# Macaron transformer block: transposes of the score maxima before or behind the products of probabilities and v

## What is computed

```python
x = x + 0.5 * ffn(layernorm(x))      # 256 -> 1024 -> 256, exact gelu, weights quantised to -1, 0, 1
x = x + attention(layernorm(x))      # 16 heads of 16, rotary positions, causal softmax
x = x + 0.5 * ffn(layernorm(x))

scores = einsum('bhqd,bhkd->bhqk', q, k) / 4;  scores = where(causal, scores, -inf)
attn = softmax(scores);  out = einsum('bhqk,bhkd->bhqd', attn, v)
```

## Time and profile before

| | us |
|---|---|
| median of 3 runs | 616.01 (614.93 to 616.15) |
| profiled execution, its own time | 616.8 |
| its span, first to last instruction | 614.8 |
| TensorE busy, matmuls | 572.6 (93% of the span) |
| VectorE busy | 459.6 (75%) |
| ScalarE busy | 344.7 (56%) |
| GpSimd busy | 231.7 (38%) |
| mean granted clock of TensorE, of full speed | 0.989 |

### The profile page before, as it was taken

How to read it: one execution, slowest core, us unless ns; L and a number is a source line. 1 busy time by engine, 2 the same in 40 slices (tenths; PEclk the granted TensorE clock), 3 DMA queues, 4 the chain that set the end, 5 groups by cost and what they waited for, 6 DMA issues and landing times. The chain is left out here.

```text
span 614.8 us, 17908 instructions
## 1 busy us (share of the span) xinstructions
PE 572.6 (93%) x6596; PEld 500.6 (81%) x6596; DVE 459.6 (75%) x928; ACT 344.7 (56%) x610; POOL 231.7 (38%) x446
## 2 busy tenths in 40 slices
PE   1999999998689999999999999999878899999997
PEld 1789989998568888888888888888765689999996
DVE  5977777787587888888888797877662677777764
ACT  2665555554326667766667666567545645555552
POOL 6383333333545463543535435434120433333310
PEclk9999999999888999999999999999999999999999
DMA  7520000002676666556666555756400010111111
GB/s 224 192 98 2 0 0 0 0 0 56 160 207 181 185 180 186 164 151 174 182 188 168 150 163 159 205 157 185 131 3 2 1 36 34 34 34 34 34 34 35
DMA packets 71142, 63.45 MB, mean 103 GB/s; under 512 B 4130, under 2 KB 64322, under 8 KB 71106
## 3 DMA queue, kind: packets, MB, share of 16 engines
q1 hardware_dynamic: 68185, 61.95, 34.8%
q10 hardware_dynamic: 2921, 1.00, 0.7%
HBM read 33.03 MB, written 29.36 MB: 101 GB/s over the span
## 5 line engine op out<-in xcount | busy, mean ns | idle before, releaser
L809 DVE TENSOR_REDUCE mx<-bank 128x2 f32<-128x512 f32 (+1 forms) x192 | 118.8, 683 | 31.6 <-PE bank L996 31.6
L522 PE MATMUL bank<-w2q,g_hi 128*128 128x256 f32 x512 | 125.0, 285 | 2.1 <-DVE g_lo L342 1.8
L437 ACT ACTIVATE g<-bank,b1c 128x512 f32<-128x512 f32 x128 | 87.9, 691 | 66.1 <-PE bank L173 60.9
L522 PE MATMUL bank<-w2q,g_lo 128*128 128x256 f32 x512 | 122.5, 280 | 0.0
L922 ACT ACTIVATE probs<-bank 128x512 f32<-128x512 f32 x192 | 111.1, 597 | 11.8 <-PE bank L996 4.0
L522 PEld LDWEIGHTS bank<-w2q,g_hi 128*128 128x128 f32 x512 | 96.3, 188 | 4.7 <-DVE g_lo L342 1.2
L522 PEld LDWEIGHTS bank<-w2q,g_lo 128*128 128x128 f32 x512 | 96.4, 188 | 0.6
L281 POOL TENSOR_TENSOR res<-res,b2h 128x1024 f32 (+1 forms) x16 | 38.3, 2395 | 144.5 <-DVE xn L147 113.2
L342 DVE TENSOR_TENSOR g_lo<-g,g_hi 128x512 fp32r<-128x512 f32 x128 | 82.6, 687 | 3.1
L173 PE MATMUL bank<-xt_hi,w1q 128*128 128x512 f32 x240 | 77.3, 404 | 3.0 <-DVE xt_lo L167 1.8
L173 PE MATMUL bank<-xt_lo,w1q 128*128 128x512 f32 x240 | 76.4, 400 | 0.0
(11 more groups left out here) (130 smaller groups left out, 1153.1 us busy)
## 6 DMA issues: line engine op xcount, KB each, us to landing
q<-qk_slots SPq DMA_DIRECT2D x32, 384.0 KB, 4.0
k<-qk_slots SPq DMA_DIRECT2D x32, 384.0 KB, 4.8
qk_slots<-parts SPq DMA_DIRECT2D x31, 384.0 KB, 3.5
qk_slots<-parts SPq DMA_DIRECT2D x31, 256.0 KB, 3.3
res<-x SPq DMA_DIRECT2D x8, 512.0 KB, 3.9
out<-res SPq DMA_DIRECT2D x8, 512.0 KB, 2.9
qk_slots<-parts SPq DMA_DIRECT2D x31, 128.0 KB, 3.2
w1f<-w1t SPq DMA_DIRECT2D x2, 512.0 KB, 6.1
```

What stands on the lines that cost most here:

```text
L437: nc.scalar.activation(g[:, f, :], of[f][:], ACT.Gelu, bias=b1c[:, f:f + 1]).then_inc(g_ready, 1)
L522: last = nc.tensor.matmul(to[:, 0:D], part[:, f, t * P:(t + 1) * P], w2q[:, f, :], start=f == 0 and part is g_hi, stop=f == FC - 1 and par ...
L809: nc.vector.tensor_reduce(o, i, AX.X, ALU.max).then_inc(s_done, 1)
```

## The change

At the end of TensorE's `step`, PV is issued ahead of MT instead of behind it. Nothing else differs, on TensorE or any other engine.

```diff
                     if p.known and p.p == BATCH - 2:
                         pe.wait_ge(s_done, UNITS * BATCH)
                         transpose_x(pe, following)
+                if p.has(0):
+                    PV(p, h)
                 if p.has(1):
                     MT(p, h)
-                if p.has(0):
-                    PV(p, h)
 
             periods(pe.Fori, step)
```

## The result

| | before | after |
|---|---|---|
| median, us | 615.47 (4 runs, 614.67 to 616.15) | 623.56 (4 runs, 621.16 to 624.06) |
| ratio | | 1.0124, 95% interval 1.0093 to 1.0155 |
| profiled execution, its own time / span | 616.8 / 614.8 | 623.15 / 621.2 |
| mean granted clock | 0.989 | 0.982 |

The change makes the kernel slower: the median is 8.1 us higher, and the ratio makes 7.6 us (5.7 to 9.5). Forecast were 4.9 us and a time of 620.9; 623.6 lies inside the range, nearer to its upper end.

What follows compares the result with a forecast made beforehand. TensorE, almost never idle, and the two-bank ring through ScalarE were taken as level, without slack. Loop 3.2, six other seams 0.5, special seams 0.2 - 0.3 + 0 + 1.3 made 4.9 us: 620.9 us, range 617.2 to 625.5.

Steps and rivals of the forecast that it cites:

- overlaps lost on ScalarE: Upper bound at the seams: ScalarE's copies take their whole lengths, making the exponential later by another 0.20 us each.
- No slack at the seam: Between two halves, a first exponential late by d makes T2, and everything behind it on TensorE, late by d.
- Step 1: TensorE alone at a seam: three changes of tile shape instead of two, costing 0.09 us a seam.
- Step 2: ScalarE's copies and exponential behind MT: first exponential 0.21 us late behind h = 0 in the loop, 0.11 behind h = 1.
- ScalarE does not overlap: Rival at the seams: ScalarE's three chained instructions take their whole lengths, 10.5 us in all, to 626.5; chance 0.13.
- Step 3: The sum over seams: 3.2 us for periods 1 to 10 in the loop, 4.9 us with all seams outside it.
- The special places: Four seams: period 0, h = 1, 0.2 us; period 13, h = 0, -0.3; period 14, 0 and 1.3.
- all of it passes on: Period 14, h = 1: TensorE already waited for the exponential, so its whole 1.3 us lateness adds to the time.
- Faster: Rival: PV fills MT's two stalls for the maxima, 2.2 us, and seams cost nothing: 613.8 us; chance 0.06.
- no change: Rival: seams free, period 14's 1.3 us set off against period 13's stall, within 1.2 us of 616.0; chance 0.07.
- the shift is mostly swallowed: Rival: the further change of shape at the seams is free, 2.3 us in all, 618.3 us; chance 0.16.
- lower bound of 2.3 us: Whole kernel with the further change of shape free: loop seams cost 0.12 and 0.02 us, sum 2.3 us.

Runs made afterwards that it cites:

- e3: Kernel after, with ScalarE's copy of the maxima moved behind the copy to `o_sb`, ahead of the exponentials: 618.04 us against 614.75, ratio 1.0046.
- e5: Kernel before, with MT called inside PV, behind its first group, wherever there is a PV: 623.62 us against 615.18, ratio 1.0139.
- e7: Kernel before, with PV ahead of MT only at the end of period 13, h = 0: 614.99 us against 615.18, ratio 0.9998.
- e1: Kernel after, but with MT still ahead of PV at the last seam (period 14, h = 1): 619.42 us against 614.75, ratio 1.0062.
- e4: Kernel after, with ten unread transposes added on TensorE between T1 and T2 of period 15: 619.57 us against 614.75, ratio 1.0077.
- e2: Kernel before, with PV ahead of MT only at the last seam (period 14, h = 1): 618.51 us against 614.75, ratio 1.0054.
- e6: Kernel after, unchanged, compared once more with the kernel before: 623.56 us against 615.18, ratio 1.0150.

## Why the prediction was right, and where it was short

The direction, the place and the two mechanisms held. That the time fell inside the range owes something to luck: 3.4 us of it come from the granted clock, which the prediction nowhere has, and they fitted because the prediction had left room above its 4.9 us for overlaps lost on ScalarE, which were not lost. Point by point, with lateness taken at the last matmul ahead of MT and PV in each half, after against before:

- *No slack at the seam.* Right: T2 is late by what the first exponential is late, 0.17 and 0.17 us. MT never waited in the loop, so PV ahead of it could gain nothing there.
- *Step 1, one more change of shape, 0.09 us.* Right: QK to PV takes 0.33 for 0.24; e3, where nothing but this is left, loses 0.086 a seam; e5, where there are two more, 0.23; and the table at e5 shows a like cost at changes without PV. PV to MT costs what PV to S0 did, as was assumed. A further exit from the 32-column tiles is a little dearer (0.14).
- *Step 2, ScalarE's chain.* Right in kind: mt to `o_sb` 0.27, `o_sb` to exponential 0.48, no idle time between them. Behind h = 0 in the loop the size was 0.13 to 0.17 for 0.21. Behind h = 1 it was 0.09 to 0.10 for 0.11 at six of ten seams, and 0.24 to 0.31 at the other four, behind periods 2, 4, 6 and 8. There the copy to `o_sb` came 0.41 to 0.47 behind the copy to `mt` (352.19 to 352.60), and 0.27 everywhere else in the loop, period 10 included (371.36 to 371.62 behind period 9). These four are the places where the hardware loop, which takes two periods a turn, goes back to its beginning, and behind period 10 it does not. So the jump of the loop on ScalarE's queue is the likely cause; no run varied it. The rival "ScalarE does not overlap" is out.
- *Step 3, the loop.* 3.2 us forecast, 3.19 measured (-1.94 to 1.25; 3.16 at the copies). That it is so close is luck: the ten seams behind h = 0 make 1.55 for 2.1, the ten behind h = 1 make 1.64 for 1.1.
- *The special places.* Period 0, h = 1: 0.2 forecast, 0.21 measured. Period 13, h = 0: a gain of 0.3 forecast, 0.17 in the kernel after and 0.17 to 0.19 in e7. PV started 0.41 us sooner in e7 and not 0.51, since it came 0.57 behind the start of `att` (429.04 to 429.61) and not 0.46, and MT behind it took back its 0.21. Period 14, h = 0: put at 0, since S3 waits for VectorE; 0.01 measured, 1.51 late behind it for 1.50 ahead. Period 14, h = 1: the exponential 1.3 us late, measured 1.29 (from 1.52 late at S3 to 2.81 late at the exponential), and T2 with it.
- *What failed: "all of it passes on".* The term of 1.3 us at the last seam was mis-sized. It took T2's longer wait as its own length and put what follows from the wait at nothing, without a reason. But TensorE, after 1.7 us without work in a stretch where it is busy for 2.87 and then 2.24 of 3.5 us, was granted half its clock for 10.2 us, and that cost 3.36 us more. With it the account closes: 0.09 and 0.21 for period 0, 3.19 for the loop, 0.34 for periods 11 and 12, -0.17 and 0.08 for period 13, 0.01, 1.30 and 3.36 for the rest make 8.4 us, of which 5.05 are what the prediction had at 4.9. The two comparisons have 7.6 (5.7 to 9.5) and 9.2 us (8.0 to 10.5). e1 takes the wait away and e4 fills it, and in both the profile shows period 15 costing nothing more than before.
- *The rivals.* "Faster" and "no change" are out, "the shift is mostly swallowed" too. The lower bound of 2.3 us is close to what e3 measures, since that kernel has the change of shape and not the chain.

The Trainium skill has the low clock on its page TensorE: Matmul & The Clock Gate, section Part 1: The HAM clock gate: the clock is half or whole by how busy TensorE has been of late. The traces agree in kind, at 466.3 us of the kernel after. The section Terms of the same page prices it as the time at the low clock times one half, which would be an estimated 5.1 us for the 10.2 us here. Period 15 lost 3.36, and the measurement decides. In part of that time TensorE waits for others, 0.90 us for `att` at 471.93, as long as before.

Still open is what, besides the wait, decides whether the low clock comes. A long wait alone does not: in period 14 of the same kernel PV waits longer than T2 does, 1.92 us, and TensorE is less busy around it, 1.58 of 3.5 us, than around T2's wait, 2.24 of 3.5. Yet the clock stays whole.

```profile
450.77 0.64 PE L1051 MATMUL bank<-probs,v_pad 128*32 128x256 f32 x8 [1.92 <-DVE att L849]
```
```profile
448.50:452.00 3.50, 1.58 (x34) 1.13 (x34) 2.09 (x7) 0.40 (x1) 2.47 (x11) 1.00 0.00 0
```

The same holds for e1, e3 and e4, each with 1.92 us there. And e2, with the same 1.71 us at T2 as the kernel after, has a mean clock of at most 0.983 in five of twelve executions, where the kernel after has it in eight of nine. Only the profiled executions tell where the low clock lies; how often it falls into period 15 is known from means alone.

## What to carry to other kernels

On an engine that is never idle a new order can only gain where the moved instruction waits; so look first whether it does, and then what stands in line behind the other engines' answer to it (here a 0.36 us copy that had lain under 1.4 us of products came to stand ahead of the exponentials). Count the changes of TensorE's tile shape in both orders: each costs about 0.1 us here, and over the 20 seams of the loop one more made 1.7 us (e3). Where a step lengthens a wait of TensorE in a stretch in which it has little to do, price the clock behind it as well, as something that may or may not come: here 1.2 us of further wait cost 3.4 us more in the profiled executions, and ten transposes that nobody reads bought them back.

## What had not been expected of the hardware

- The granted clock fell to half 0.4 to 0.8 us behind a wait of 1.71 us (after, e2, e6) and stayed there for 10.2 us, in which TensorE was busy for 3.10 of 4 and 4.78 of 5 us (after). In the kernel before, T2's wait of 0.53 us and PV's of 0.90 behind it left it whole. A wait of 0.92 us at T2 in e5 was followed by a low clock 2.5 us later, and a wait of 1.92 us in period 14 (after, e1, e3, e4) was not followed by one.
- Ten useless transposes (1.31 us) ahead of T2 made period 15 shorter by 3.4 us.
- The two copies of ScalarE behind each other start 0.27 us apart, but 0.41 to 0.47 at the four seams at which the hardware loop goes back to its beginning, with nothing between them in the program, in each of after, e1, e4 and e6.
